# Both self attentions of a two-layer perceiver kernel: value products of one tile set between the output products of another

## The reference

```python
# twice: latent cross attention, self attention, feed forward
x = x + xattn(norm(x), ctx)         # L0x, L1x
x = x + attn(norm(x))               # L0a, L1a
x = x + ffn(norm(x))                # L0f (Hadamard FFN), L1f (32 experts, top 8)

def attn(h):                        # 16 heads of 32, causal over the 32 rows of a sequence
    q, k, v = h @ Wq, h @ Wk, h @ Wv
    ...                             # L0a: biases, 2 kv heads; L1a: 16 kv heads, q and k normed and turned by rope
    p = softmax(mask(q @ k.T / sqrt(32)))
    return (p @ v) @ Wo
```

## Time and profile before

| what | value |
|---|---|
| median of 3 runs | 2290.68 us |
| the profiled execution's own time | 2287.49 us |
| its span, first to last instruction | 2285.7 us |
| PE busy | 2118.2 us, 93% of the span |
| PE weight loads busy | 1430.8 us, 63% |
| VectorE / ScalarE / GpSimd busy | 1169.6 / 773.6 / 995.4 us |
| mean granted TensorE clock | 0.961 of full speed |
| L0a on PE | from 461.8 to 623.0 us of the span |
| L1a on PE | from 1522.4 to 1722.1 us |

### The profile page before, as it was taken

One profiled execution on the slowest core, in us unless ns is written; L12 is line 12 of the kernel. 1 busy time (PEld: TensorE's weight loads), 2 busy tenths in 40 slices (PEclk: granted clock), 3 DMA queues, 4 the chain that ended last, 5 costly groups with the idle time before them and its releaser, 6 DMA issues.

```text
span 2285.7 us, 27993 instructions
## 1 busy us (share of the span) xinstructions
PE 2118.2 (93%) x8810; PEld 1430.8 (63%) x8810; DVE 1169.6 (51%) x2688; ACT 773.6 (34%) x1962; POOL 995.4 (44%) x953
## 2 busy tenths in 40 slices
PE   7998999999888999999997999998994999999995
PEld 5865766577557864566664666656773555555552
DVE  4226777645634112355554777758765343444443
ACT  2124433323231110133334433434422444445451
POOL 1027465312237210177767475447511444455552
PEclk8998999999999999999999999998985999999998
DMA  3231001110021100011122010110033799988886
GB/s 115 83 110 54 19 26 35 31 61 1 19 92 37 50 33 0 0 51 51 39 72 88 18 28 21 67 63 1 1 129 135 244 300 303 265 216 210 221 210 163
DMA packets 84545, 209.21 MB, mean 92 GB/s; under 512 B 13857, under 2 KB 39969, under 8 KB 76929
## 3 DMA queue, kind: packets, MB, share of 16 engines
q1 hardware_dynamic: 61680, 153.54, 19.7%
q0 software_dynamic: 21280, 51.38, 11.0%
q10 hardware_dynamic: 1440, 2.49, 0.3%
HBM read 257.95 MB, written 34.36 MB: 128 GB/s over the span
## 4 chain that ended last, share of the span: by engine, by line
PE 52%; DVE 9%; ACT 4%; POOL 3%; issue 2%; DMA 1%; SPq 0%; POOLq 0%; ACTq 0%; DVEq 0%
PE banks L98 32%; PE banks L854 4%; PE banks L2204 3%; PE banks L2205 3%; DVE L1x_prob L541 2%; ACT L1x_prob L489 2%; PE banks L2179 2%; DVE L1x_small L528 1%; DVE L1x_pT_lo L509 1%; PE banks L448 1%; PE banks L1299 1%; POOL L1a_part_s L1541 1%; POOL L1a_tiny L1515 1%; PE banks L2169 1%; PE banks L1689 1%
## 5 line engine op out<-in xcount | busy, mean ns | idle before, releaser
L98 PE MATMUL banks<-L1f_w,L1f_xT 128*128 x760 | 264.1, 491 | 2.1 <-ACT L1f_xT L2272 1.1
L2453 POOL DMA_INDIRECT moe_sums<-L1f_y,L1f_row x95 | 150.7, 1586 | 220.5 <-DVE L1f_is_who L2325 153.9
L159 POOL TENSOR_TENSOR rstd<-rstd,power 128x1 f32<-128x1 f32 x48 | 30.0, 624 | 368.6 <-DVE rstd L153 368.6
L98 PEld LDWEIGHTS banks<-L1f_w,L1f_xT 128*128 128x128 f32 x760 | 137.8, 191 | 81.6 <-issue 6.2
L2461 POOL DMA_INDIRECT L1f_xg<-moe_rows,L1f_row x95 | 94.2, 991 | 73.9 <-DVE L1f_row L2320 47.7
L448 PE MATMUL banks<-L0x_wn,L0x_qT 128*128 128x512 f32 x256 | 115.1, 593 | 0.8 <-DVE x L518 0.8
L448 PE MATMUL banks<-L1x_wn,L1x_qT 128*128 128x512 f32 x256 | 115.1, 593 | 0.8 <-DVE x L518 0.8
L2292 DVE SCALAR_TENSOR_TENSOR L1f_z<-banks,L1f_share,L1f_sg 128x192 f32<-128x192 f32 x95 | 39.7, 418 | 146.4 <-ACT L1f_sg L2227 146.4
L489 ACT ACTIVATE L0x_prob<-banks,L0x_small 128x256 f32<-128x256 f32 x128 | 59.0, 472 | 159.9 <-DVE L0x_small L531 159.9
L489 ACT ACTIVATE L1x_prob<-banks,L1x_small 128x256 f32<-128x256 f32 x128 | 59.0, 472 | 158.1 <-DVE L1x_small L531 158.1
L98 PE MATMUL banks<-L0f_down,L0f_z 128*128 128x512 f32 x256 | 111.1, 592 | 1.5 <-DVE L0f_z L1787 1.5
(11 more groups left out here) (389 smaller groups left out, 5353.9 us busy)
## 6 DMA issues: line engine op xcount, KB each, us to landing
L1f_w<-in_experts SPq DMA_DIRECT2D x95, 1280.0 KB
L1f_laid<-moe_counts SPq DMA_DIRECT2D x59, 512.0 KB, 5.4
w<-in_L1x_heads SPq DMA_DIRECT2D x16, 704.0 KB, 4.1
w<-in_L0x_heads SPq DMA_DIRECT2D x16, 608.0 KB, 3.7
w<-in_wug SPq DMA_DIRECT2D x8, 1024.0 KB, 4.8
L0x_craw<-in_ctx SPq DMA_DIRECT2D x96, 64.0 KB, 2.0
L1x_craw<-in_ctx SPq DMA_DIRECT2D x96, 64.0 KB, 2.0
w<-in_L0x_out SPq DMA_DIRECT2D x4, 1280.0 KB, 6.4
```

The costliest lines, as they stand in the source:

```text
L98: ins = pe.e.matmul(out, w, m, start=first and n == 0, stop=last and n == len(pairs) - 1)
L2453: pool.e.indirect_dma_start(self.sums[j % 2][:, :], bass.IndirectOffsetOnAxis(ap=self.row[:, j:j + 1], axis=0), self.y[j % self.NY][:], No ...
```

## The change

Both self attentions (one class) and the head of the Hadamard FFN are reordered; no arithmetic is added or removed.

- On PE `turn_weights(i-4)` goes to the front of the iteration, ahead of `score(i-3)`, and so does the next stage's `turn_early`.
- `mix` comes one iteration sooner: iteration i mixes tile i-4 instead of i-5. Its 16 products are set between the four matmuls of the output of tile i-5: output part 0, 6 products, part 1, 5 products, part 2, 5 products, part 3 (`mix_and_output`).
- The tables of bank uses follow the new order. With it scores always land in one of the two mixing banks and mixed values in the other, so `mix_free` of the values of tile i-4 waits for `o_set` of tile i-5.
- ScalarE copies the turned weights ahead of the softmax exponential. VectorE's order stays, but for the last tile: `keep_mixed(7)` goes to iteration 11, behind the softmax sums.
- In the Hadamard FFN `fold_down` uses banks 3 and 4 instead of 4 and 5, waits for the end of the attention's q, k, v and of its turned weights instead of for the whole attention, and starts ahead of `transform_rows(6)`. ScalarE's copies of the folded weights go ahead of `rows_hi` and `keep_rows` of the last tiles. VectorE's last steps swap places.

```diff
         self.mix_use = {}
         for i in range(NT + 5):
             if 0 <= i - 3 < NT:
                 self.mix_use["scores", i - 3] = len(self.mix_use)
-            if 0 <= i - 5 < NT:
-                self.mix_use["values", i - 5] = len(self.mix_use)
+            if 0 <= i - 4 < NT:
+                self.mix_use["values", i - 4] = len(self.mix_use)
...
+            self.after.turn_early(pe, i)
+            if 0 <= i - 4 < NT:
+                self.turn_weights(pe, i - 4)
             if 0 <= i - 3 < NT:
                 self.score(pe, i - 3)
-            if 0 <= i - 5 < NT:
-                self.mix(pe, i - 5)
             if 0 <= i - 2 < NT:
                 self.spread(pe, i - 2)
-            if 0 <= i - 4 < NT:
-                self.turn_weights(pe, i - 4)
-            if self.after:
-                self.after.turn_early(pe, i)
-            if 0 <= i - 5 < NT:
-                self.project_out(pe, i - 5)
-            if self.after:
-                self.after.ask_early(pe, i)
+            self.mix_and_output(pe, i - 4, i - 5)
+            self.after.ask_early(pe, i)
...
+    MIXED_TO = (0, 6, 11, AT * BPT, AT * BPT)
+
+    def mix_and_output(self, pe, i, o):
+
+        if 0 <= i < NT:
+            self.mix_free(pe, "values", i)
+            pe.wait_ge(self.vbd_act, 8 * i + 8)
+            pe.wait_ge(self.vbd_dve, 8 * i + 8)
+        if 0 <= o < NT:
+            self.bank7_free(pe, "output", o)
+            self.w[3].landed(pe)
+            pe.wait_ge(self.o_set, o + 1)
         for t in range(AT):
...
+            if 0 <= o < NT:
+                ins = pe.e.matmul(self.sh.psum(7), self.oTb[o % 2][:, t, :], self.w_o[:, t, :], start=t == 0, stop=t == AT - 1)
+                if t == AT - 1:
+                    ins.then_inc(self.projected.sem, 1)
+            if 0 <= i < NT:
+                pe.wait_ge(self.pT_set, i + 1)
+                for n in range(self.MIXED_TO[t], self.MIXED_TO[t + 1]):
+                    self.mix(pe, i, *divmod(n, BPT))
...
-            if 0 <= i - 5 < NT:
+            if 0 <= i - 5 < NT - 1:
                 self.keep_mixed(dve, i - 5)
...
+            self.after.rows_early(dve, i)
+            if 0 <= i - 3 < NT:
+                self.sum_weights(dve, i - 3)
+            if i - 4 == NT - 1:
+                self.keep_mixed(dve, i - 4)
+            if 0 <= i - 5 < NT:
+                self.add_output(dve, i - 5)
...
     def tensor(self, pe):
         self.turn_rows(pe, NT - 2)
+        self.fold_down(pe, 0)
         self.transform_rows(pe, NT - 2)
-        self.begin(pe)
-        self.fold_down(pe, 0)
         self.turn_rows(pe, NT - 1)
         self.fold_down(pe, 1)
         self.transform_rows(pe, NT - 1)
         for q in range(2, FC // 4):
             self.fold_down(pe, q)
+        self.begin(pe)
         self.widen_and_down(pe)
...
     def scalar(self, act):
-        self.rows_hi(act, NT - 3)
-        self.keep_rows(act, NT - 2)
-        self.rows_hi(act, NT - 2)
-        self.begin(act)
         for q in range(FC // 4):
             for n in range(4 * q, 4 * q + 4):
                 act.wait_ge(self.down_mixed, n + 1)
-                act.e.copy(self.down[:, n, :], self.sh.psum(4 + n % 2)).then_inc(self.down_kept.sem, 1)
-            if q == 1:
-                self.keep_rows(act, NT - 1)
-            elif q == 2:
-                self.rows_hi(act, NT - 1)
+                act.e.copy(self.down[:, n, :], self.sh.psum(3 + n % 2)).then_inc(self.down_kept.sem, 1)
+            if q < 3:
+                self.rows_hi(act, NT - 3 + q)
+            if q < 2:
+                self.keep_rows(act, NT - 2 + q)
+        self.begin(act)
```

More of the change, by code:

```diff
@@ L1288, in turn_weights, with mix @@
         ins.then_inc(self.p_turned.sem, 1)
[L1290 to L1295, removed]
-        for t in range(AT):
[L1297 to L1308, removed]
+    MIXED_TO = (0, 6, 11, AT * BPT, AT * BPT)
[8 more added lines that the diff above has]
+            pe.wait_ge(self.o_set, o + 1)
+        for t in range(AT):
+            if 0 <= o < NT:
[6 more added lines that the diff above has]
+                    self.mix(pe, i, *divmod(n, BPT))
+    def mix(self, pe, i, t, b):
+        at = t * P + b * S
+        ins = pe.e.matmul(self.mix_bank("values", i)[:, at:at + S], self.vbd[i % 3][:, b, t // self.tpg, :],
+                          self.pTb[i % 2][:, t, b * S:(b + 1) * S], start=True, stop=True)
+        if (t, b) == (AT - 1, BPT - 1):
+            ins.then_inc(self.mixed.sem, 1)
     def scalar(self, act):
@@ L1318, in scalar @@
                 self.input_hi(act, i + 1)
+            t = i - 4
+            if 0 <= t < NT:
+                act.wait_ge(self.p_turned, t + 1)
+                act.wait_ge(self.mixed, t - 1)
+                act.e.copy(self.pTb[t % 2][:].rearrange("p t n -> p (t n)"), self.turn_bank("p", t)).then_inc(self.pT_set.sem, 1)
             if 0 <= i - 3 < NT:
@@ L1324, in scalar @@
                 self.spread_act(act, i - 2)
-            t = i - 4
-            if 0 <= t < NT:
-                act.wait_ge(self.p_turned, t + 1)
-                act.wait_ge(self.mixed, t - 1)
-                act.e.copy(self.pTb[t % 2][:].rearrange("p t n -> p (t n)"), self.turn_bank("p", t)).then_inc(self.pT_set.sem, 1)
-            if self.after:
-                self.after.keep_early(act, i)
+            self.after.keep_early(act, i)
     def by_batch(self, ap):
@@ L1546, with __init__ @@
 class HadamardFfn(Stage):
[L1549 removed]
+    def __init__(self, sh, name, number, left, arena, left_early, left_turning):
         super().__init__(sh, number, left)
[L1551 removed]
+        self.name, self.left_early, self.left_turning = name, left_early, left_turning
         self.after = None
@@ L1623, in rows_early @@
     def rows_early(self, dve, i):
+        for t in self.EARLY.get(i - 1, ()):
+            self.scale_rows(dve, t)
         for t in self.EARLY.get(i, ()):
             self.normalise(dve, t)
-        for t in self.EARLY.get(i - 1, ()):
-            self.scale_rows(dve, t)
         for t in self.EARLY.get(i - 2, ()):
@@ L1685, in fold_down @@
         w.landed(pe)
+        self.begin_early(pe)
+        for signal, n in self.left_turning:
+            pe.wait_ge(signal, n)
         for a in range(4):
@@ L1688, in fold_down @@
             pe.wait_ge(self.down_kept, n - 1)
-            pe.e.matmul(self.sh.psum(4 + n % 2), self.had[:, 1, :], w.ap[:, a * D:(a + 1) * D], start=True,
+            pe.e.matmul(self.sh.psum(3 + n % 2), self.had[:, 1, :], w.ap[:, a * D:(a + 1) * D], start=True,
                         stop=True).then_inc(self.down_mixed.sem, 1)
@@ L2480, in build_kernel @@
         first.after = stage(SelfAttention, "L0a", KVH, False, first.mixed_all)
-        first.after.after = stage(HadamardFfn, "L0f", first.after.projected_all)
+        first.after.after = stage(HadamardFfn, "L0f", first.after.projected_all, first.after.turned_all)
         second = first.after.after.after = stage(RotatedQueries, "L1x", first.after.after.widened)
```

36 lines of the change are left out of this document (15 added, 21 removed).

## The result

The changed kernel is slower: 2341.8 us (median of 4 runs, 2340.06 to 2343.5) against 2291.27 us of the kernel before in the same job (2289.09 to 2292.04), a ratio of 1.0222 [1.0204, 1.024], or 50.5 us. The forecast was 2295.7 us with a range up to 2308. The profiled execution took 2343.5 us.

The account below looks back on a forecast made before the run. PE was taken as the bound, busy 93% of the span, so only idle time and clock could change. L1a +6.6 and L0a with head -1.6 gave +5.0 us: 2292.5 for the profiled execution, 2295.7 as median, range 2280 to 2308.

Parts of the forecast that it names:

- the new waits: Both attentions: PE idles before the first output matmul for VectorE's copy; net of waits removed, L1a +13.0, L0a +7.3 us.
- how often the clock falls: Half-speed stretches behind new holes: 4.5 in L1a (+8.6 us), 2.5 in L0a and the FFN's head (+4.8 us).
- A stretch at half speed costs 1.9 us: Price per clock loss behind a hole, from 4 fold records taking 3.78 us against 4 x 0.46.
- The clock holds: Rival, both attentions: new holes too short to cost clock, except the two longest (+3.8 us); 2284 to 2286 us, chance 0.3.
- The sign it was to be known by: Signs in the trace, among them L1a iterations of 22.3 us instead of 19.94 and holes before the first output matmul.
- The wide bound of that paragraph: Upper bound of the clock cost behind new holes: all seventeen lose the clock, +32 us.
- the clock regained: Both attentions: the finely mixed sequence keeps 2.4 GHz where long value-product runs lost it; at most -8.1 (L0a), -15.0 us (L1a).
- alternation itself gains nothing: Value products between output matmuls: one weight load hides under each large matmul in either order; 0, at best 3.8 us won.
- the mixed sequence itself loses the clock: Rival: the alternated output and value products lose clock by themselves, 14 blocks x 1.9 = 27 us; 2319 us, chance 0.04.
- The head: Hadamard FFN's head, turn at 623.00 to first wide product: 23.3 instead of 28.95 us, -5.6 (bounds -2 and -9).
- none of the four: Four rivals: clock holds (chance 0.3), clock falls at nearly each hole (0.17), head gains nothing (0.07), mixed sequence loses clock (0.04).
- The clock falls at nearly each hole: Rival: twelve half-speed stretches behind holes instead of seven, +5 x 1.9 us, so +14.5; 2305 us, chance 0.17.

Follow-up runs that it names:

- The block order: The changed kernel with its holes, but the four output matmuls first and the 16 value products behind them in one block: 2299.79 us, ratio 1.0029.
- the run with the copy in the same iteration: The changed kernel with VectorE's copy of a tile's mixed values in the iteration that mixes it, ahead of the output's addition: 2259.58 us, ratio 0.9854.
- the last pair: The changed kernel with the copy in the iteration that mixes: alternated order 2259.58 us, four output matmuls first and value products in one block 2260.64 us.
- the fastest version: The changed kernel with VectorE's copy of mixed values in the iteration that mixes them, alternated order kept: 2259.58 us, ratio 0.9854.

## Why the prediction was wrong

**Right: the new waits.** Their cause (`keep_mixed` behind `mask_scores`), their places and nearly their sizes came: forecast 1.9 us, 2.3 us and 3.3 us for the steady iterations and L1a's iteration 10, measured 1.68, 2.19 and 3.22; forecast 5.8 and 7.2 us for L1a's iterations 5 and 8, measured 4.11 and 6.30. Idle time rose by 8.5 us in L1a, where the sum had +13.0, and by 4.2 in L0a, where it had +7.3. These terms were 7.6 us too high.

**Right in the main: how often the clock falls.** Seven stretches were forecast, 4.5 for L1a and 2.5 for L0a and the head; eight came in the attentions, six of them in L1a, and a short one in the head, in the four folds from 643.61 that took 5.26 us instead of 3.7. The 2.19 us holes fell three times of three, where half was assumed.

**Wrong: what one costs.** The step that failed is "A stretch at half speed costs 1.9 us". It was read from four records of the fold, 128x512 matmuls one behind the other. The sentence against the rival "The clock holds", that small products stand in the hole's neighbourhood, was used for the chance and not for the price. Behind these holes the half level lasted the whole sequence or nearly so: 5.0 to 6.7 us, and up to 8.2 with the q products. The block order shows 0 to 1.7 us behind the same 2.19 us, and the head's folds 1.6, so 1.9 is a fair price where wide matmuls follow; the price belongs to what follows a hole. The eight sequences cost 47.6 us, where the sum had 13.4 for seven: with these prices the forecast would have been 2295.7 + 34 = 2330, most of the way to 2341.8. The sign it was to be known by says the same: L1a iterations of 22.3 us were forecast, 29.8 came (1643.37 to 1673.16), and the mean clock of L1a was 0.77. Even the range's upper bound, which reached to a few stretches more at the same price, could not cover it. The wide bound of that paragraph, all seventeen at 1.9 us (+32), was too low for the same reason.

**Half right: the clock regained.** -8.1 and -15.0 us were forecast if the value products no longer lose it. The changed kernel hides this, but the run with the copy in the same iteration shows some of it: L1a's busy time falls by 3.9 us (182.04 to 178.19), and by about 10 without its one half-speed sequence, where 15.0 were forecast. L0a's falls by 7.4 us (150.41 to 143.06); that this is near the forecast is luck, since L0a of before was a favourable draw (157.97 in the run with the head alone). And the reason was wrong. In L0a of the kernel before none of the eight value blocks lost the level, each took 3.65 to 3.76 us; what ran slow there were output matmuls, for one those of iteration 8, 4.87 us where 3.6 is full speed:

```profile
567.45 4.87 PE L98 MATMUL banks<-w,L0a_oTb 128*128 128x512 f32 x8
```

In L1a three of eight blocks lost it, the slowest at 5.44 us. And the block order of the last pair regains as much as the alternated one: L0a's mean clock is 0.98, and 15 of its 16 value blocks take 3.5 to 3.7 us from start to next. So it isn't fineness. That the value products stand beside wide matmuls, and no longer between scores and transposes, is what both orders share; no run tries it alone, and the cause of what was regained stays open.

**Right: alternation itself gains nothing** in loads: 2259.6 against 2260.6 us, 2274.9 against 2272.9, and 7.01 against 6.92 us for one sequence. The Trainium skill, "TensorE: Matmul & The Clock Gate", section "The mechanism", has PE pull weight loads ahead of matmuls in flight. The 3.8 us that the prediction estimated from this for the alternated order do not show in these runs.

**Right to reject: the mixed sequence itself loses the clock.** (Its 2319 us is 27 us on top of the profiled execution's 2292.5; on the forecast's own basis it is 2322.) L0a runs it at a mean clock of 0.99 where no hole is in front. The Trainium skill, "TensorE: Matmul & The Clock Gate", section "A second HAM failure mode: psum-queue depth-cycling", ties a loss of clock to cycling through PSUM banks in each iteration, with short idle times of PE between groups of matmuls. Here six changes in a sequence cost nothing without a hole, and with holes the number of changes does not order the times.

**The head** was sized -5.6 us; -4.4 in the changed kernel, -9.4 [-12.6, -6.4] alone, -5.9 in the fastest version's trace. The sum took VectorE's chain as the bound of it. The stretch took 24.2 to 24.7 us in all five kernels with L0a's holes, and 20.3 to 23.0 in the five that have the new head and few or none; that the holes delay VectorE's chain fits this and is not shown by itself.

**The rival that came** was none of the four as priced. "The clock falls at nearly each hole" had the mechanism (2305 us, chance 0.17), with the price that was wrong for all.

What stays open: the cause of the clock regained; what sets iteration 7 of L0a apart, which lost the level behind 1.67 us where its neighbours kept it behind as much, and what in the sequence lets the level fall only after a first matmul at full speed. The runs give counts for it, not a rule.

## What to carry to other kernels

When a reordering puts a wait in front of PE, price the wait by its own length and by what PE does behind it, from a row with the same kind of work behind a hole: here 2.2 us of idle time cost up to 1.7 us more in front of four 512-column matmuls, and some 6 to 8 us more in front of a mix of wide matmuls and small, load-bound products. Put dense work directly behind a wait that can't be removed. And when a consumer moves one iteration earlier, move the copy it waits for on the other engine too: the place was there, 1.6 us of idle time on VectorE, and it turned +2.2% into -1.5%. And before comparing stages of single profiled executions, profile one kernel's stage twice: the same order of PE in L0a came out 7 us apart.

## What the runs showed of the hardware

- At 1.2 GHz from its start (1643.37 in the changed kernel), PE did not get back to 2.4 GHz in 13 us of unbroken work in which one 512-column output matmul stood between each 5 or 6 value products (each a 128x128 weight load and 32 columns). It came back among the wide q products behind it: in the changed kernel these take 0.63 us apiece from 1657.53 and 0.39 from 1660.78. Entered at 2.4 GHz and without a hole in front, the same sequence stays there: L0a of the fastest version, mean clock 0.99 over 148 us.
- The fall can come later than the hole: after 1.67 and 2.19 us of idle time the first output matmul was still at full speed (1.12 and 1.13 us for its two records), and the small products behind it lost the level.
- The same program order with the same hole of 2.19 us came out at 3.70 us in one iteration and 5.40 in another. A single hole's price is not fixed.
- With the same order of PE two executions passed L0a at mean clocks of 0.95 and 0.90, in 161.2 and 168.5 us.
